# Two steps of the values product as one TensorE job, in a transformer block whose order of work a planner writes

## The reference

```
mod = (silu(c) @ wmod).reshape(16, 6, 1, -1)          # sa, ca, ga, sb, cb, gb
h = layernorm(x) * (1 + ca) + sa
Q, K, V = h @ q_w.T + q_b, h @ k_w.T + k_b, h @ v_w.T + v_b      # 16 heads of 16
scores = Q K^T / 4 + slope[h] * (pos_k - pos_q), -inf where pos_k > pos_q
x = x + ga * (softmax(scores) @ V @ o_w.T + o_b)
h = layernorm(x) * (1 + cb) + sb
x = x + gb * fp4_linear(silu(fp4_linear(h, w_gate)) * fp4_linear(h, w_up), w_down)
```

## Time and profile before

| | |
|---|---|
| median of 3 runs | 3654.35 us |
| profiled execution, span from the first to the last instruction | 3655.0 us |
| TensorE busy | 3495.8 us, 96% |
| VectorE busy | 2984.2 us, 82% |
| ScalarE busy | 1976.6 us, 54% |
| GpSimd busy | 1269.8 us, 35% |
| instructions | 57026 |

### The profile page before, as it was taken

The page is one execution under the profiler, slowest core; times in us unless marked ns, Lnnn a source line. Parts: engine busy times, 40 slices in busy tenths (PEclk is TensorE's granted clock), DMA queues, the critical chain, the costliest instruction groups (busy, mean ns, idle before and its releaser), DMA issues.

```text
span 3655.0 us, 57026 instructions
## 1 busy us (share of the span) xinstructions
PE 3495.8 (96%) x20920; PEld 1876.0 (51%) x20920; DVE 2984.2 (82%) x5836; ACT 1976.6 (54%) x3629; POOL 1269.8 (35%) x919
## 2 busy tenths in 40 slices
PE   6989999999999999999999999999999999999987
PEld 2334554555555555554555555555554545555455
DVE  9988878788887888878788887888878788887755
ACT  3555555555555555555555555555555565555631
POOL 5214334242342524334242342524334242432233
PEclk7899999999999999999999999999999999999998
DMA  7262323333242332423333242332423333232100
GB/s 127 43 102 36 68 51 62 62 49 65 46 71 42 62 66 39 68 51 62 62 50 65 46 71 42 62 65 39 70 49 65 59 51 67 43 59 42 25 26 12
DMA packets 160938, 205.34 MB, mean 56 GB/s; under 512 B 44740, under 2 KB 100628, under 8 KB 160660
## 3 DMA queue, kind: packets, MB, share of 16 engines
q1 hardware_dynamic: 160660, 201.69, 32.2%
HBM read 63.65 MB, written 17.89 MB: 22 GB/s over the span
## 4 chain that ended last, share of the span: by engine, by line
PE 83%; DVE 11%; ACT 4%; issue 2%; POOL 1%; DMA 0%; SPq 0%; POOLq 0%; ACTq 0%; DVEq 0%
PE banks L742 14%; PE banks L766 13%; PE banks L724 12%; PE banks L863 8%; PE banks L870 8%; PE banks L886 7%; PE banks L793 6%; PE banks L844 3%; PE banks L824 3%; ACT arena L954 3%; PE banks L879 2%; PE banks L727 2%; DVE banks L1191 2%; DVE top L1189 1%; PE banks L771 1%
## 5 line engine op out<-in xcount | busy, mean ns | idle before, releaser
L954 ACT ACTIVATE arena<-banks 128x512 f32<-128x512 f32 (+1 forms) x2432 | 1268.3, 580 | 814.2 <-PE banks L724 508.5
L1191 DVE CUSTOM_DVE_ANT_0 banks<-banks,mask 128x640 f32<-128x640 f32 (+3 forms) x1024 | 1034.9, 1044 | 267.8 <-PE banks L766 263.2
L724 PE MATMUL banks<-qa,ka 105*128 105x512 bf16 (+3 forms) x3072 | 785.5, 328 | 19.3 <-ACT arena L954 15.9
L766 PE MATMUL banks<-ka,qa 102*128 102x512 bf16 (+3 forms) x3072 | 758.8, 332 | 29.7 <-DVE top L1189 20.1
L742 PE MATMUL banks<-arena,va 128*17 128x512 f32 (+3 forms) x6144 | 645.2, 492 | 8.5 <-ACT arena L954 7.6
L1088 POOL TENSOR_TENSOR hid<-hid,tm 128x704 f32<-128x704 f32 x128 | 214.7, 1678 | 972.3 <-DVE hid L1165 972.3
L724 PEld LDWEIGHTS banks<-qa,ka 105*128 105x128 bf16 x3072 | 272.5, 97 | 432.4 <-ACT arena L954 173.8
L766 PEld LDWEIGHTS banks<-ka,qa 102*128 102x128 bf16 x3072 | 254.7, 99 | 409.2 <-issue 87.5
L1189 DVE TENSOR_REDUCE top<-banks 128x2 f32<-128x768 f32 (+3 forms) x384 | 391.5, 1042 | 43.8 <-PE banks L771 41.5
L886 PE MATMUL banks<-wdT,hqT 128*128 128x256 f32 x1536 | 368.1, 390 | 4.3 <-ACT hqT L997 4.3
L886 PEld LDWEIGHTS banks<-wdT,hqT 128*128 128x128 f32 x1536 | 295.2, 195 | 76.9 <-ACT arena L954 13.6
(11 more groups left out here) (152 smaller groups left out, 4625.8 us busy)
## 6 DMA issues: line engine op xcount, KB each, us to landing
qa<-parts SPq DMA_DIRECT2D x384, 128.0 KB, 4.6
ka<-parts SPq DMA_DIRECT2D x384, 128.0 KB, 6.6
xa<-in_x SPq DMA_DIRECT2D x16, 1024.0 KB, 5.3
xr<-in_x SPq DMA_DIRECT2D x64, 256.0 KB, 2.7
out_x<-xr SPq DMA_DIRECT2D x64, 256.0 KB, 2.2
rsumT<-rsum_dram SPq DMA_DIRECT2D x63, 256.0 KB
onT<-oT SPq DMA_DIRECT2D x252, 64.0 KB, 2.6
ffn_rows<-rows_dram SPq DMA_DIRECT2D x16, 256.0 KB, 3.2
```

The lines of the kernel that those rows point to most:

```text
L724: mm = pe.matmul(ps[:, m * w:(m + 1) * w], ka[g][0:KT, h, kt * P:(kt + 1) * P], qa[g][0:KT, h, q0:q0 + w], start=heads < G and m == 0, sto ...
L766: mm = pe.matmul(ps[:, at:at + z - a], qa[g][0:KS, h0 + m, qt * P:(qt + 1) * P], ka[g][0:KS, h0 + m, a:z], start=qt > 0 and m % paired == ...
L954: nc.scalar.activation(probs[:, s % P_SLOTS, j * heads:(j + 1) * heads, 0:w], ps[:, 0:heads * w].rearrange("p (h q) -> p h q", h=heads), A ...
L1191: nc.vector.tensor_tensor_reduce(out=ps, in0=ps, in1=mask[:, S - w:S], scale=1.0, scalar=MASKED, op0=ALU.add, op1=ALU.max, accum_out=tops) ...
```

## The change

A PV job now takes two steps, an even one and the odd one after it: it waits for the exponentials of the second, then issues the four matmuls of the first and the four of the second. `pv_done` counts pairs (six for each group, `TURNS`), so every wait on it is rewritten: ScalarE's copy out, the values' copy of the next batch, and the exponentials' wait for their slot, which now waits for the pair that holds the step three back. The output bank is opened by the first pair. No matmul is added or taken away.

The planner gets a state, the array's tiling (1 for all jobs, 4 for PV), and starts a TensorE job 0.095 us later where it differs from the one before. The assumed costs of many jobs are changed by some per cent, up to a fifth, and `SHIFT` is another table with larger values and more kinds of jobs, so the order of work on every queue is another one.

```diff
+TURNS = NS // 2
...
-    SHIFT = {"ACT CO": 12.0, "ACT GA": -28.0, "ACT HT": -16.0, "ACT T": -11.0, "ACT TR": 22.0, "ACT U": 11.0,
...
+    SHIFT = {"ACT CO": 42.0, "ACT GA": -43.0, "ACT HT": -8.0, "ACT KROW": 78.0, "ACT LX": 22.0, "ACT T": -74.0,
...
+             "PE V": -1.0, "PE WD": 2.0, "PE WT": 1.0, "PE XT": 14.0, "POOL FOLD": -33.0, "POOL HIGH": 150.0,
+             "POOL HQ": -21.0, "POOL MID": -35.0, "POOL MUL": -3.0, "POOL OB": 105.0, "POOL RES": 62.0, "POOL REST": -40.0,
+             "POOL SPL": 50.0, "POOL WG": -61.0, "POOL XQ": 22.0, "SP DEN": 58.0, "SP DOWN": 5.0, "SP FGATE": 162.0,
+             "SP FROW": -2.0, "SP GROW": -100.0, "SP MOVE": -36.0, "SP NUM": 46.0, "SP OUT": -42.0, "SP RBC": 56.0,
+             "SP RDW": -21.0, "SP TOP": 57.0, "SP XA": -3.0, "SP XIN": -30.0}
...
+        mode = 1
...
+                if key[0] == "PE" and MODE.get(key[1][0], 1) != mode:
+                    t += SWITCH
...
+            if engine == "PE":
+                mode = MODE.get(event[0], 1)
...
+MODE = {"PV": 4}
+SWITCH = 0.095
...
-                       takes_cost=0.17 + 0.833e-3 * w * heads,
-                       then=(("PE", ("PV", old // (NG * NS), old // NS % NG, old % NS)),) if i == 0 else ())
+                       takes_cost=0.125 + 0.833e-3 * w * heads,
+                       then=(("PE", ("PV", old // (NG * NS), old // NS % NG, old % NS | 1)),) if i == 0 else ())
...
-                p.add("PE", ("PV", b, g, s), 1.9e-3 * w + 0.03, due + 3, ("ACT", ("T", b, g, s, jobs_of(s) - 1)),
-                      ("PE", ("PV", b, g, s - 1)) if s else None, ("ACT", ("V", b, 1)) if (g, s) == (0, 0) else None, lag=0.22,
-                      banks=1 if s in FIRST else 0, holder=("ACT", ("CO", b, g, c)) if s in FIRST else None)
+                if s % 2:
+                    first = s - 1 in FIRST
+                    p.add("PE", ("PV", b, g, s), 1.69e-3 * (w + span(s - 1)[1]) + 0.02, due + 3, ("ACT", ("T", b, g, s, jobs_of(s) - 1)),
+                          ("PE", ("PV", b, g, s - 2)) if s > 1 else None, ("ACT", ("V", b, 1)) if (g, s) == (0, 1) else None, lag=0.22,
+                          banks=1 if first else 0, holder=("ACT", ("CO", b, g, c)) if first else None)
...
-            p.add("DVE", ("XQ", b, r), 2.75, due + 4, ("DVE", ("XR", b, r)), ring="Q")
-            p.add("POOL", ("XQ", b, r), 2.6, due + 6, ("DVE", ("XQ", b, r)), takes="Q")
+            p.add("DVE", ("XQ", b, r), 3.2, due + 4, ("DVE", ("XR", b, r)), ring="Q")
+            p.add("POOL", ("XQ", b, r), 2.35, due + 6, ("DVE", ("XQ", b, r)), takes="Q")
...
-                        kt, c = STEPS[s]
-                        q0, w = span(s)
-                        if s in FIRST:
+                        if s - 1 in FIRST:
                             open_banks(e)
-                        out = bank(("PV", b, g, FIRST[c]))[:, q0 - c * BANK:q0 - c * BANK + w]
-                        if g == 0 and s == 0:
+                        if g == 0 and s == 1:
                             pe.wait_ge(a_free, in_a["V", b, 1])
                         pe.wait_ge(a_free, in_a["T", b, g, s, jobs_of(s) - 1])
-                        for h in range(G):
-                            mm = pe.matmul(out[32 * h:32 * h + VW, :], va[:, kt, g * G + h, :],
-                                           probs[:, s % P_SLOTS, h, 0:w], start=s in FIRST,
-                                           stop=s in LAST, skip_group_check=True)
+                        for step in (s - 1, s):
+                            kt, c = STEPS[step]
+                            q0, w = span(step)
+                            out = bank(("PV", b, g, FIRST[c] + 1))[:, q0 - c * BANK:q0 - c * BANK + w]
+                            for h in range(G):
+                                mm = pe.matmul(out[32 * h:32 * h + VW, :], va[:, kt, g * G + h, :],
+                                               probs[:, step % P_SLOTS, h, 0:w], start=step in FIRST,
+                                               stop=step in LAST, skip_group_check=True)
                         mm.then_inc(pv_done, 1)
...
-                        act.wait_ge(pv_done, n * NS + LAST[c] + 1)
+                        act.wait_ge(pv_done, n * TURNS + (LAST[c] + 1) // 2)
...
-                            act.wait_ge(pv_done, b * NG * NS)
+                            act.wait_ge(pv_done, b * NG * TURNS)
...
-                        if j == 0 and (b * NG + g) * NS + s >= P_SLOTS:
-                            act.wait_ge(pv_done, (b * NG + g) * NS + (s - P_SLOTS + 1))
+                        old = (b * NG + g) * NS + s - P_SLOTS
+                        if j == 0 and old >= 0:
+                            act.wait_ge(pv_done, old // 2 + 1)
```

More of the change, by code:

```diff
@@ L265, in maxima @@
                      + [("DVE", ("QROW", b, g)), ("ACT", ("KROW", b, g))] if j == 0 else ()),
-                   ring="D", on="DVE", takes_cost=(0.2 if w <= BANK else 0.33) + 1.042e-3 * w * heads, banks=-(-heads * tile_pitch(heads, w) // BANK),
+                   ring="D", on="DVE", takes_cost=(0.14 if w <= BANK else 0.29) + 1.042e-3 * w * heads, banks=-(-heads * tile_pitch(heads, w) // BANK),
                    then=(("DVE", ("SM", b, g - 1) if g else ("SM", b - 1, NG - 1)),) if j == 0 else ())
@@ L270, in maxima @@
             old = ("MT", b, g - 1) if g else ("MT", b - 1, NG - 1)
-            p.add("DVE", ("SM", b, g), 1.5, due, ("DVE", ("S", b, g, NT - 1)), ("DVE", old))
+            p.add("DVE", ("SM", b, g), 1.05, due, ("DVE", ("S", b, g, NT - 1)), ("DVE", old))
             older = ("TOP", b, g - 2) if g >= 2 else ("TOP", b - 1, g + 2)
@@ L313, in normalise @@
         if g % 2:
-            p.add("POOL", ("MUL", b, g // 2, *half), 2.4, due + 10.0, *(("SP", (k, b, g - 1)) for k in ("NUM", "RBC")),
+            p.add("POOL", ("MUL", b, g // 2, *half), 2.45, due + 10.0, *(("SP", (k, b, g - 1)) for k in ("NUM", "RBC")),
                   *(("SP", (k, b, g, *half)) for k in ("NUM", "RBC")), lag=8.0)
@@ L351, in feed_forward @@
             pe(("O", b, r), 1.75, at + 2.0 + r, ("POOL", ("MUL", b, 0)), ("POOL", ("MUL", b, 1, *half)), ("POOL", ("WG", b)),
-               ring="D", on="DVE", takes_cost=2.0, then=(("POOL", ("FOLD", b, r)), ("DVE", ("LN", b - 1, NPAIR - 1))))
+               ring="D", on="DVE", takes_cost=1.75, then=(("POOL", ("FOLD", b, r)), ("DVE", ("LN", b - 1, NPAIR - 1))))
         for half in (0, 1) if b == HALVED[0] else ((),):
             mine = range(NPAIR) if half == () else (2 * half, 2 * half + 1)
-            p.add("DVE", ("LR", b) if half == () else ("LR", b, half), 2.4, at + 6.0, *(("DVE", ("O", b, r)) for r in mine))
+            p.add("DVE", ("LR", b) if half == () else ("LR", b, half), 2.1, at + 6.0, *(("DVE", ("O", b, r)) for r in mine))
         first, every = at + 0.06 * L, 0.235 * L
@@ L360, in feed_forward @@
             tile = lambda t: (b, t) if t >= 0 else (b - 1, t + T)
-            p.add("ACT", ("LX", b, r), 1.2, due - 2, ("DVE", ("LR", b, r // 2) if b == HALVED[0] else ("LR", b)), ("ACT", ("WT", 0, GU // 2)), ("ACT", ("WD", 0, C - 1, 1)), ("PE", ("XT", *pair(-2))),
+            p.add("ACT", ("LX", b, r), 1.1, due - 2, ("DVE", ("LR", b, r // 2) if b == HALVED[0] else ("LR", b)), ("ACT", ("WT", 0, GU // 2)), ("ACT", ("WD", 0, C - 1, 1)), ("PE", ("XT", *pair(-2))),
                   ("DVE", ("HQ", *tile(2 * r - 3))))
-            p.add("DVE", ("LN", b, r), 1.4, due, ("ACT", ("LX", b, r)), ("SP", ("FROW", b)))
-            p.add("DVE", ("XR", b, r), 1.35, due + 2, ("DVE", ("LN", b, r)), ("DVE", ("XQ", *pair(-1))))
-            p.add("DVE", ("XQ", b, r), 2.75, due + 4, ("DVE", ("XR", b, r)), ring="Q")
-            p.add("POOL", ("XQ", b, r), 2.6, due + 6, ("DVE", ("XQ", b, r)), takes="Q")
+            p.add("DVE", ("LN", b, r), 1.53, due, ("ACT", ("LX", b, r)), ("SP", ("FROW", b)))
+            p.add("DVE", ("XR", b, r), 1.38, due + 2, ("DVE", ("LN", b, r)), ("DVE", ("XQ", *pair(-1))))
+            p.add("DVE", ("XQ", b, r), 3.2, due + 4, ("DVE", ("XR", b, r)), ring="Q")
+            p.add("POOL", ("XQ", b, r), 2.35, due + 6, ("DVE", ("XQ", b, r)), takes="Q")
             pe(("XT", b, r), 0.55, due + 8, ("POOL", ("XQ", b, r)), ("PE", ("UP", *tile(2 * r - 3))),
@@ L373, in feed_forward @@
                        ("PE", ("GA", b, t, 0)) if k else (("PE", ("GA", b, t - 1, 1)) if t % 2 else None),
-                       ring="A", on="ACT", takes_cost=1.8 if 2 * (t % 2) + k in (0, 3) else 0.5,
+                       ring="A", on="ACT", takes_cost=1.75 if 2 * (t % 2) + k in (0, 3) else 0.46,
                        lock=((b, r), t % 2 == 1 and k == 1))
                 pe(("UP", b, t), 2.4, late + 2, ("PE", ("GA", b, t, 1)), ("PE", ("UP", *tile(t - 1))), ring="D", on="DVE",
-                   takes_cost=0.95, banks=2, then=(("ACT", ("GA", b, t, 1)),))
-                p.add("DVE", ("HR", b, t), 1.75, late + 4, ("DVE", ("UP", b, t)), ("DVE", ("HQ", *tile(t - 1))))
```

(6 more changed lines are left out.)

21 lines of the change are left out of this document (7 added, 14 removed), and 5 rows, old and new, of the table SHIFT.

## The result

The changed kernel takes 3688.56 us (median; 3685.26 to 3693.48), the kernel before 3653.82 us beside it. The ratio is 1.0098, with an interval of 1.0083 to 1.0112: slower by 35 us, where 84 us of gain were forecast. The forecast missed by 118 us, on the wrong side of no change and outside its range.

The account below looks back on a forecast made before the run. TensorE was taken to set the pace in steady batches. Saving 84 us on PV jobs, with moved waits and the rebuilt order at nothing, gave 3655 - 84 = 3571 us (chance 0.50), range 3535 to 3620.

Parts of the forecast that it names:

- What the edit saves: TensorE's PV jobs: 768 become 384, 0.22 us saved for each of 381 pairs, 84 us, or 5.3 us a batch.
- Rival 4: Inside the pair job: second step's weight loads are paid in the open, gain only 34 us, 3621 us; chance 0.03.
- What bounds the kernel now: Steady batches: TensorE, busy 214.55 of 219.04 us, sets the pace, so time taken out of its stream counts fully.
- rival 1: VectorE: bursts like its xb work beside GpSimd's multiplication eat half of the gain, 3613 us; chance 0.17.
- The rebuilt order: All queues: 9 us loss set against planner's moves, sum taken at nothing; the run's two ends 10 us each way.
- SyncE's order: SyncE's queue: a transfer behind a waiting one could be 6.6 us late, but taken at nothing.
- rival 5: Whole run: merging works, but the new order loses 5 us per batch, for instance by collisions; 3650 us; chance 0.05.
- The slots: ScalarE's tighter wait before odd steps' exponentials: some 2 us spare in each pair, cost nothing, upper end 111 us.
- Rival 3: Exponentials wait for slots held by pairs, ScalarE's queue stands and TensorE waits: slower, 3682 us; chance 0.08.
- The closing test: Forecast is wrong if PV records and their starts are as said and the batch period is still above 216 us.

Follow-up runs that it names:

- e5: Kernel before, order untouched, with the mask matmuls of T jobs with fewer than four heads left out and mask tiles zeroed: 3607.82 us (0.988).
- e14: Changed kernel with the mask matmuls of T jobs with fewer than four heads left out: 3678.07 us (1.007).
- e7: Changed kernel with only SyncE's order altered, DEN moved ahead of NUM and one MOVE: 3658.41 us (1.0014).
- e1: Kernel before, single PV jobs and order kept, with only ScalarE's slot wait before odd steps' exponentials tightened: 3653.98 us (1.000).
- e2: Kernel before with its planned order, each even step's PV matmuls issued in front of the odd step's: 3711.58 us (1.0162).

## Why the prediction was wrong

**What the edit saves was right**, in every term: 0.09 + 0.13 us for a job that stands alone, the second entry free, 382 places, 5.3 us a batch. Rival 4 (weight loads in the open) fell with the duration of the pairs, and in the timeline above four of the second step's loads (by count the ninth to twelfth of sixteen) stand at 1644.79, while the first step's matmuls still run.

**The step that failed first is the one under "What bounds the kernel now": "whatever is taken out of its own stream is worth its full length, as long as nobody else becomes late".** TensorE's busy share of 98% in a batch was read as the bound. But e5 took the same 5.3 us out of TensorE without moving a thing, and 55% of it arrived. My reading, which no run isolates: T and S jobs, their readers and the banks form a loop, and part of TensorE's 98% was a stream that happened to be just long enough to cover that loop. With nothing else moved, half of the saving was to be expected, 3655 − 46 = 3609. That is close to rival 1's number by luck, as rival 1 gave other grounds. In the changed order the share is 12% (e14), at most 30% with the clock set aside. The other side of this account, from the pages' totals: in the version with DEN and slots mended the split took VectorE from 2980.7 to 2940.0 us and the time fell by 43; in the changed kernel it went from 2993.7 to 2943.0 and the time fell by 54; in the kernel before, short REST took VectorE from 2984.2 to 2954.6 and gave 6. So the bound moved: in the new order a microsecond of these VectorE instructions is worth about one, of TensorE one to three tenths; in the old it was a fifth and a half. (What a microsecond of VectorE is worth includes the clock that TensorE gets back.)

**"The rebuilt order … I take the sum at nothing" was wrong by about 84 us, in two terms.** SyncE's order was taken as nothing, because "TensorE waited for no transfer in a steady batch". That is a statement on the order of before, and the prediction's list of what moves on SyncE leaves out DEN and NUM. DEN's due time went from -1 to +58 and NUM's from -1 to +46, the new values are in the diff, and the term cost 30 us (e7). Not TensorE but VectorE waited, and TensorE behind it. Collisions with GpSimd were rival 1's and rival 5's mechanism, and it is what happened, but as a burst of xb work "once a batch", at 1.4 us each; REST cost 54 us in the new order against 6 before. Their sum over VectorE is not much larger than before: what VectorE instructions take above their usual shortest time rose by only 1.4 us a batch, and short REST saves VectorE 30 us in the old order and 44 in the new (2980.7 to 2936.9). What changed is which instructions REST meets: before it left those on hid and on xb of line 1285 (1268 before) alone, as the groups above show, and now it meets them, with TensorE standing at the end of the same queue. I argue, and no run isolates it, that before it fell where VectorE had slack. The prediction had no term for the clock either: it read 1.00 in a steady batch and left it there.

**The slots**: the slack computed was right for the old order (e1, single jobs: no loss; e2, pairs: 3.6 us of ScalarE's standing) and nearly so for the new (8 to 11 us, of an upper bound of 111). Rival 3 named the wait that then stood out most in the profile, 508.5 us, and it was the smallest of the three causes. Its price was idle time of ScalarE, which isn't the path.

**The account of the 118 us** between 3571 and 3688.6: DEN's place 30, slots 11, REST's meetings 54, each taken on top of the one before; the run without these three, at 3592.6, is still 22 above the forecast. By the argument above, not by a run, that is the part of TensorE's time that isn't on the path (that run also leaves out REST's work on 896 columns, so the 22 are a lower bound). The edit alone, without a new order, would not have brought the forecast either: e2 shows that in the old order pairing costs 58 us.

**The closing test** of the prediction ("wrong if the records and their starts are as said and the period is still above 216") is met as written. Open is why exactly e2's order loses 9.2 us a batch: its many short waits are shown and the slots are ruled out, the spacing that single PV jobs gave is my reading of them, and no run restored the spacing alone. Open too is how much of each cause is its waits and how much the clock that they bring down, as no run holds the clock.

## What to carry to other kernels

A busy share of 98% doesn't say that the engine's time is worth its length: take some of it out in place, without moving anything, and see what arrives, before pricing an edit with it. Where an order is rebuilt, go through every queue for transfers that now stand behind others, a queue that only issues included, and look at which engine reads what they bring. Where VectorE meets a long GpSimd instruction, issue the latter in pieces; and judge a wait by who stands behind it, not by its total. Look at the granted clock in steady batches of both kernels: here it fell behind short stands of TensorE where it had been full.

## What the runs showed of the hardware that was not expected

A VectorE instruction that reads two SBUF operands stood for the rest of the GpSimd instruction beside it, as in this pair of rows of the timeline of the kernel after, where an instruction that takes 0.69 us as a rule (the median of its 64, here and in the split version) takes 2.67 beside one of 2.14.

```profile
1913.53 2.14 POOL L1074 TENSOR_TENSOR xa<-xa,parts 128x1024 f32<-128x1024 f32 x1
1913.55 2.67 DVE L1285 TENSOR_TENSOR xb<-xb,ffn_rows 128x512 f32<-128x512 f32 x1
```

That the wait ends with the GpSimd instruction, not with the GpSimd work, is the useful part. Four instructions of 801 ns in place of one of 2164 cost GpSimd 42% more time (197.2 for 138.5 us) and let VectorE in between them: the longest of these VectorE instructions fell from 2.67 to 1.75 us. The Trainium skill (SBUF — State Buffer, Who interferes with whom) states that a VectorE instruction with two SBUF inputs and a GpSimd instruction that reads SBUF exclude each other for the whole instruction; these rows agree.

Entering the column-tiled mode and leaving it cost TensorE 0.22 us together, in pairs as in single jobs: the pair of 512s above starts 0.15 us after a mask matmul that otherwise takes 0.06, and takes 1.84 to the next start, which within 0.01 is 1.72 of columns (8 x 0.215, half of 0.77 - 0.34) and 0.13. The second step's weight loads cost the pair nothing, though its four tiles have the same rows as the first's.

After TensorE had stood 1.6 to 2.2 us behind VectorE, its granted clock was 0.50 for 3.4 us, eight times in twelve batches of the kernel after, and a pair in such a stretch took 3.13 us in place of 1.84. Where the same wait was at most 0.6 us (the split alone, above), the steady batches stayed at full clock.
